# Row gathers of a graph network: no bound on the index, and no clearing of the row buffers

## The chip, the cores and the metric

The kernel runs on one core of a Trainium2 chip. The metric is device time in microseconds (us), and less is better. Engines are named as the profile names them: PE is TensorE (PEld its weight loads), DVE is VectorE, ACT is ScalarE, POOL is GpSimd and SP is SyncE; a q behind a name means that engine's sequencer.

## What is computed

Four graph layers run one after the other over 50,000 nodes of 128 features, each followed by an addition of its input and a layer norm. The edges are 25,000 random pairs in both directions, plus one loop edge per node, 100,000 in all and sorted by destination. Each layer sums rows of neighbours:

```
x = layernorm(x + gcn(x))        # two rounds:  out = D^-1/2 (A + I) D^-1/2 (x W) + b
x = layernorm(x + sage(x))       # three rounds: h W_self + mean(h[src]) W_neigh + b
x = layernorm(x + attention(x))  # sum of messages[src] * sigmoid(logit), then a GRU cell, then a batch norm
x = layernorm(x + combine(x))    # sum(x[src]) W_neigh + x W_self + b
# every sum over neighbours:  segment_sum(table[src], dst)
```

What matters here is `table[src]`: seven times, rows of a table in HBM are fetched for the 50,000 edges that are no loops. A row has 128 floats (512 B), but 256 floats (1024 B) in the second sage round and 132 floats (528 B) in the attention.

## The kernel before

**Slots.** `sort_edges` (L301) gives each of the edges that is no loop a slot. Four groups of 512 nodes make a supergroup of 2048 nodes (SG = 4); there are 25 supergroups, the last with two groups. A supergroup has K = 17 columns of 128 slots. The first 1024 edges of a supergroup fill columns 0 to 7 from the front (HALF = 8), and the rest fill columns from 16 downwards, so that what stays unfilled in a full supergroup lies in column 8 or next to it. With 2048 edges per supergroup in the mean, column 8 is nearly empty. The last supergroup uses columns 0 to 7 only. That makes 24 x 17 + 8 = 416 columns, 53,248 slots for 50,000 edges.

Of each slot, `idx` holds the row to fetch and `dcol` the node within the column's window. An unfilled slot gets no match in `dcol`, so its one-hot column is zero and whatever row lies in it is multiplied by zero. Before the change, L567 marks the unfilled slots and L570 adds NOWHERE (2^20) to their index, which is past the table's end.

**Gather stages.** Seven stages use the class `EdgeRows` (L602): `gcn_first` (tiles named g_, table t_x), `gcn_second` (g_, t_h), `sage_first` (s_, t_x), `sage_second` (s_, t_h, 256 wide), `sage_third` (s_, t_v), `attend` (at_, t_m) and `combine` (cb_, t_x). Between two stages all engines meet in a barrier (L254). In each stage:

- DVE copies the indices of the next batch into a small tile (`aim`, L646) and makes the one-hot tiles (L683), in the order of `over_groups` (L121), four groups ahead of the sums (three in the split stages, two in `attend`);
- POOL waits for that copy and issues one indirect DMA per column (`gather`, L655): 5, 5, 4 and 3 columns for the four groups of a supergroup. Each fetches 128 rows, one into each partition;
- PE multiplies rows and one-hots into a PSUM bank (L720), and the dense work of the layer follows.

The rows land in a ring of K column buffers. Stages with whole fp32 rows have two such rings (34 columns), the two split stages (`gcn_first` and `sage_second`, which part the rows into a high and a low half) one. Since a skipped row leaves the buffer as it was, DVE clears all rings at the start of a stage (`clear`, L633, called by `on_vector` at L700), and POOL waits for `cleared` before it first writes each ring. The indirect DMA is given `bounds_check=NPAD - 1` (L659), and skips rows beyond it. The bound stands in a register of POOL's sequencer, which a MOVE writes ahead of each gather.

Of the kernel before, what the change touches and what calls it, by code (L numbers as in the profile page):

```python
# [14 lines left out]
ALU = mybir.AluOpType  # L15
# [11 lines left out]
NPAD = T * GRP  # L27
LAST = NODES - (T - 1) * GRP
LASTP = LAST // BLK
SG = 4  # L30
SGN = SG * GRP
NSG = -(-T // SG)
K = 17
# [14 lines left out]
NOWHERE = 1 << 20  # L48
# [41 lines left out]
def is_first(t, slots=2):  # L90

    return isinstance(t, int) and t < slots


def wait_for(eng, sem, value):


    eng.wait_ge(sem, value)  # L98
    if not isinstance(value, int):
        eng.sem_inc(PASSED[0], 1)  # L100
# [24 lines left out]
def over_groups(eng, stages, unroll=8):  # L125


    lim = T - 2

    def step(s):  # L130
        for lag, stage in stages:
            if 0 <= s - lag < T:
                stage(Turn(None, unroll, s - lag))

    most = max(lag for lag, _ in stages)
    head = max(2 + most, unroll)
    head += (T - 2 - head) % unroll
    for s in range(head):
        step(s)
    with eng.Fori(0, (lim - head) // unroll) as j:  # L140
        for o in range(unroll):
            for lag, stage in stages:
                stage(Turn(j, unroll, head + o - lag))
    for s in range(lim, T + most):
        step(s)
# [17 lines left out]
def build_program(nc, x, src, dst, w1, b1, w2, b2, ws0, wn0, sb0, ws1, wn1, sb1, ws2, wn2, sb2,  # L163
# [4 lines left out]
    def sb(name, shape, dt=F32):  # L168
        return top.enter_context(nc.sbuf_tensor(name, shape, dt))
# [28 lines left out]
    dcol = sb("dcol", [P, SLOTS])  # L198
# [45 lines left out]
    class Phase:  # L244


        def __init__(self, ctx, name):
            self.ctx, self.name, self.own_sems = ctx, name, []
            ctx.callback(self.clear)

        def clear(self):

            nc.clear_and_free_semaphores(self.own_sems)
            nc.all_engine_barrier()  # L254
# [46 lines left out]
    def sort_edges():  # L301
# [3 lines left out]
        with ExitStack() as ctx:  # L305
            ph = Phase(ctx, "so")
# [16 lines left out]
            a, b, c = (tmp(f"a{i}", [P, CW]) for i in range(3))  # L323
# [11 lines left out]
            filled = tmp("filled", [P, SLOTS])  # L335
# [99 lines left out]
            def _(dve):  # L435
                steps = [0]

                def then(ins):

                    steps[0] += 1  # L440
                    ins.then_inc(chain, 1)
                    dve.wait_ge(chain, steps[0])

                flat = [t[:, :, :].rearrange("p b i -> p (b i)")
                        for t in (si, di, ni, sf, df, nf, ends, coded, scrap)]
# [23 lines left out]
                                         op0=ALU.mult, op1=ALU.add).then_inc(marked, 1)  # L469
# [10 lines left out]
                                              op0=ALU.mult, op1=ALU.add))  # L480
# [5 lines left out]
                                              op0=ALU.is_equal, op1=ALU.mult))  # L486
# [7 lines left out]
                                              op0=ALU.mult, op1=ALU.add))  # L494
                then(dve.scalar_tensor_tensor(out=c[:, :], in0=c[:, :], scalar=float(SGN), in1=bound[:, :],
                                              op0=ALU.add, op1=ALU.subtract))
                for n, what in enumerate((s_t, c)):
# [33 lines left out]
                                              op0=ALU.mult, op1=ALU.add))  # L531
# [3 lines left out]
                                              op0=ALU.mult, op1=ALU.add))  # L535
# [24 lines left out]
                for n in (0, 2):  # L560
# [3 lines left out]
                v = sums[:, :, :, :].rearrange("p n s f -> p (n s) f")[:, 0:SLOTS, :]  # L564
                dve.scalar_tensor_tensor(out=dsg[:, :], in0=v[:, :, 3], scalar=256.0, in1=v[:, :, 2],
                                         op0=ALU.mult, op1=ALU.add)
                dve.tensor_scalar(filled[:, :], v[:, :, 3], 0.0, None, ALU.is_equal)  # L567
                then(dve.scalar_tensor_tensor(out=dcol[:, :], in0=v[:, :, 1], scalar=256.0, in1=v[:, :, 0],
                                              op0=ALU.mult, op1=ALU.add))
                then(dve.scalar_tensor_tensor(out=dcol[:, :], in0=filled[:, :], scalar=float(NOWHERE),  # L570
                                              in1=dcol[:, :], op0=ALU.mult, op1=ALU.add))
                dve.tensor_scalar(dsg[:, :], dsg[:, :], 256.0, None, ALU.subtract)
                then(dve.tensor_scalar(dcol[:, :], dcol[:, :], 256.0, 0.0, ALU.subtract, ALU.max))
                then(dve.tensor_copy(idx[:, :], dcol[:, :]))
# [4 lines left out]
                def table(tile):  # L579
# [5 lines left out]
                                              op0=ALU.is_ge, op1=ALU.mult))  # L585
# [16 lines left out]
    class EdgeRows:  # L602
# [3 lines left out]
        def __init__(self, ph, table, width, split=False):  # L606
            self.table, self.width = table, width
            self.rings = 1 if split else 2
            self.rows = ph.tile("rows", [P, self.rings * K, width])
            if split:  # L610
                self.hi, self.lo = ph.tile("hi", [P, K, width], F32R), ph.tile("lo", [P, K, width], F32R)
            self.halves = split
            self.onehot = ph.tile("onehot", [P, K, WMAX], F32R if split else F32)
            self.index = ph.pair("index", [P, BATCHMAX], U32, n=2 * SG)
            self.cleared = ph.sem("rows_cleared")
            self.indexed = ph.sem("index_copied")
            self.gathered = ph.sems("rows_gathered", 2 * SG)
            self.split = ph.sem("rows_hi")
            self.ready = ph.sem("rows_ready")
            self.summed = ph.sem("rows_summed")  # L620
# [9 lines left out]

            return K * (q.e // SG) if self.rings == 2 else 0

        def clear(self, dve):  # L633

            for n in range(self.rings):
                dve.memset(self.rows[:, n * K:(n + 1) * K, :], 0.0).then_inc(self.cleared, 1)  # L636

        def aim(self, dve, q):

# [7 lines left out]

        def gather(self, pool, q):

            if is_first(q.t, self.rings * SG):  # L650
                pool.wait_ge(self.cleared, q.t // SG + 1)
            wait_for(pool, self.indexed, q.t + 1)
            a, b = self.batch(q)
            for k in range(a, b):
                pool.indirect_dma_start(  # L655
                    out=self.rows[:, self.ring(q) + k, :], out_offset=None, in_=self.table[0:NPAD, :],
                    in_offset=bass.IndirectOffsetOnAxis(ap=self.index[q.e][:, k - a:k - a + 1], axis=0),
                    bounds_check=NPAD - 1, oob_is_err=False).then_inc(self.gathered[q.e], 16)

        def fetch(self, pool):  # L660

# [38 lines left out]
        def on_vector(self, dve, stages, ahead=None):  # L700


            ahead = ahead or (3 if self.halves else 4)
            self.clear(dve)
            over_groups(dve, [(0, lambda q: self.aim(dve, q))] +
                        [(ahead + lag, stage) for lag, stage in stages])

# [1486 lines left out]
```

## Time and profile before

| | |
|---|---|
| median of 3 runs | 5997.48 us (5992.59 to 5998.52) |
| the profiled execution | 5996.4 us, span of its instructions 5994.6 us |
| busy share: PE, PEld, DVE, ACT, POOL | 80%, 63%, 65%, 45%, 52% |
| indirect DMAs | 7 x 416 = 2912 |
| bytes of POOL's DMA queue | 205.88 MB |
| mean granted TensorE clock | 0.928 of full |

Times in the rows are microseconds from the span's start unless they are marked ns. In a row of the timeline, the first number is the start and the second the duration; in brackets stands how long the engine was idle before it and what ended that. "issue" means that the engine waited for nothing that the profile shows.

### The profile page before, as it was taken

Reading aid. Unit: us, or ns where it says so; the run is one execution under the profiler, and the core shown is the slowest. Engines: PE = TensorE matmul, PEld = TensorE weight load, DVE = VectorE, ACT = ScalarE, POOL = GpSimd, SP = SyncE. Lnnn points to the kernel's source line nnn. Section 1 sums busy time; section 2 is a strip of 40 time slices with the busy share of each in tenths; the row PEclk is TensorE's granted clock in tenths of the full one; section 3 lists DMA queues with packets and bytes.
Section 4 is the critical chain, followed back from the end, with each engine's and each line's share of the span. In section 5 each row is a group of like instructions: output and inputs, shape, how many; then the busy total and the mean of one; then the engine's idle time right before and its main releaser. Section 6 shows DMA issues by size and latency. Waiting matters only on the chain. (4 is left out here: it accounts for less than half of the span.)

```text
span 5994.6 us, 107473 instructions
## 1 busy us (share of the span) xinstructions
PE 4806.3 (80%) x27114; PEld 3769.5 (63%) x27114; DVE 3884.4 (65%) x11826; ACT 2702.2 (45%) x6502; POOL 3119.7 (52%) x2957
## 2 busy tenths in 40 slices
PE   2208999566589998999999997777699999546887
PEld 1106888455478886777777775677566666326777
DVE  9805777566666664555555554788577777785666
ACT  0083544455622222222222222666566666694545
POOL 0007776677677754343433433777555554005776
PEclk9999999777799998999999998999899999657999
DMA  1096898444467764444444442777555555594444
GB/s 31 9 333 209 267 272 262 127 139 137 136 193 222 222 209 141 148 154 144 150 152 143 154 147 88 179 191 190 172 162 153 162 156 149 189 305 131 145 142 134
DMA packets 523175, 1010.93 MB, mean 169 GB/s; under 512 B 110803, under 2 KB 118082, under 8 KB 519962
## 3 DMA queue, kind: packets, MB, share of 16 engines
q1 hardware_dynamic: 423194, 803.47, 41.0%
q0 software_dynamic: 99840, 205.88, 14.2%
q8 instruction: 52, 0.85, 0.1%
q14 instruction: 89, 0.73, 0.0%
HBM read 686.75 MB, written 335.49 MB: 171 GB/s over the span
## 5 line engine op out<-in xcount | busy, mean ns | idle before, releaser
L655 POOL DMA_INDIRECT s_rows<-t_h,s_index x416 | 536.8, 1290 | 849.0 <-DVE s_index L646 747.9
L655 POOL DMA_INDIRECT g_rows<-t_x,g_index x416 | 444.5, 1069 | 579.9 <-DVE g_index L646 455.8
L655 POOL DMA_INDIRECT cb_rows<-t_x,cb_index x416 | 416.0, 1000 | 471.4 <-DVE cb_index L646 347.1
L655 POOL DMA_INDIRECT at_rows<-t_m,at_index x416 | 442.0, 1062 | 405.4 <-DVE at_index L646 300.8
L720 PE MATMUL bank<-s_onehot,s_rows 128*128 128x80 f32 (+9 forms) x2344 | 478.4, 358 | 154.7 <-DMA s_rows<-t_v,s_index 124.6
L720 PEld LDWEIGHTS bank<-s_onehot,s_rows 128*128 128x128 f32 x2344 | 410.4, 204 | 216.0 <-issue 89.3
L655 POOL DMA_INDIRECT s_rows<-t_v,s_index x416 | 422.6, 1016 | 214.9 <-issue 124.0
L655 POOL DMA_INDIRECT g_rows<-t_h,g_index x416 | 428.4, 1030 | 168.2 <-issue 122.2
L655 POOL DMA_INDIRECT s_rows<-t_x,s_index x416 | 425.0, 1022 | 161.4 <-issue 114.1
L720 PE MATMUL bank<-g_onehot,g_rows 128*128 128x80 f32 (+9 forms) x1172 | 307.0, 428 | 217.0 <-DMA g_rows<-t_h,g_index 194.4
L1606 DVE TENSOR_TENSOR s_rout<-bank,s_x 128x512 f32<-128x512 f32 x98 | 67.8, 692 | 586.0 <-PE bank L1550 586.0
L720 PEld LDWEIGHTS bank<-g_onehot,g_rows 128*128 128x128 f32 x1172 | 255.3, 249 | 273.1 <-issue 166.2
L1550 PEld LDWEIGHTS bank<-wuv_s,s_hid 128*128 128x128 f32 x3136 | 365.5, 192 | 47.4 <-issue 47.4
L683 DVE TENSOR_SCALAR s_onehot<-iota,dcol 128x224 f32<-128x224 f32 (+15 forms) x1248 | 380.4, 368 | 0.6
L1573 ACT ACTIVATE s_hid<-bank,sb_c 128x512 f32<-128x512 f32 x196 | 123.9, 683 | 568.3 <-PE bank L1538 568.3
L1538 PE MATMUL bank<-s_ht,ws_s 128*128 128x512 f32 x784 | 368.8, 593 | 0.0
L1538 PE MATMUL bank<-s_agg,wn_s 128*128 128x512 f32 x784 | 368.4, 592 | 0.0
L1550 PE MATMUL bank<-wuv_s,s_hid 128*128 128x128 f32 x3136 | 366.0, 275 | 0.9 <-DVE s_rout L1606 0.9
L720 PE MATMUL bank<-cb_onehot,cb_rows 128*128 128x80 f32 (+9 forms) x1172 | 244.5, 363 | 106.8 <-DMA cb_rows<-t_x,cb_index 105.2
L720 PE MATMUL bank<-g_onehot,g_hi 128*128 128x112 f32 (+9 forms) x586 | 173.1, 332 | 184.0 <-DVE g_lo L690 178.4
L720 PE MATMUL bank<-s_onehot,s_hi 128*128 128x80 f32 (+9 forms) x1172 | 288.4, 287 | 26.9 <-DVE s_lo L690 22.9
L720 PEld LDWEIGHTS bank<-cb_onehot,cb_rows 128*128 128x128 f32 x1172 | 209.1, 207 | 137.8 <-issue 74.6
(314 smaller groups left out, 12710.9 us busy)
## 6 DMA issues: line engine op xcount, KB each, us to landing
s_scale<-inv_d SPq DMA_DIRECT2D x196, 256.0 KB
t_h<-s_hout SPq DMA_DIRECT2D x98, 512.0 KB
s_own<-t_h SPq DMA_DIRECT2D x98, 512.0 KB
t_m<-s_mout SPq DMA_DIRECT2D x98, 264.0 KB
at_own<-t_m SPq DMA_DIRECT2D x98, 264.0 KB
t_x<-sx_out SPq DMA_DIRECT2D x98, 256.0 KB
g_own<-t_x SPq DMA_DIRECT2D x98, 256.0 KB
g_scale<-dinv_d SPq DMA_DIRECT2D x98, 256.0 KB
```

The source lines that it names most:

```text
L655: pool.indirect_dma_start(out=self.rows[:, self.ring(q) + k, :], out_offset=None, in_=self.table[0:NPAD, :], in_offset=bass.IndirectOffset ...
L683: last = dve.tensor_scalar(self.onehot[:, k, 0:WIDE[k]], iota[:, 0:WIDE[k]], col(dcol, q.m * K + k), None, ALU.is_equal)
L720: last = pe.matmul(to[:, a:b], part[:, at, h * P:(h + 1) * P], self.onehot[:, k, off:off + b - a], start=(i + s == 0), stop=(close and i + ...
L1538: last = pe.matmul(bank[4 + o][:, :], w[:, h, o * P:(o + 1) * P], r[q.u][:, h, :], start=(k + h == 0), stop=(k + h == 2))
L1550: last = pe.matmul(bank[6 + w][:, b * D:(b + 1) * D], hid[q.u][:, h, b * P:(b + 1) * P], wuv_s[:, h, w * D:(w + 1) * D], start=(h == 0), s ...
L1573: last = act.activation(hid[q.u][:, h, :], bank[4 + h][:, :], ACT.Relu, bias=sb1_c[:, h:h + 1])
L1606: dve.tensor_tensor(rout[q.u][:, :], bank[6][:, :], xin[q.u][:, :], ALU.add)\
```

## The change

The bound is taken off the indirect DMA, and with it everything that it needed: the two DVE operations that mark unfilled slots and push their index past the end, the clearing of the rings at the start of each of the seven stages, and POOL's wait for it. The index of an unfilled slot is now 0 (L573 takes the larger of the decoded value and 0), so row 0 of the table is fetched for it. Its one-hot column is zero as before.

```diff
                 dve.scalar_tensor_tensor(out=dsg[:, :], in0=v[:, :, 3], scalar=256.0, in1=v[:, :, 2],
                                          op0=ALU.mult, op1=ALU.add)
-                dve.tensor_scalar(filled[:, :], v[:, :, 3], 0.0, None, ALU.is_equal)
                 then(dve.scalar_tensor_tensor(out=dcol[:, :], in0=v[:, :, 1], scalar=256.0, in1=v[:, :, 0],
                                               op0=ALU.mult, op1=ALU.add))
-                then(dve.scalar_tensor_tensor(out=dcol[:, :], in0=filled[:, :], scalar=float(NOWHERE),
-                                              in1=dcol[:, :], op0=ALU.mult, op1=ALU.add))
                 dve.tensor_scalar(dsg[:, :], dsg[:, :], 256.0, None, ALU.subtract)
                 then(dve.tensor_scalar(dcol[:, :], dcol[:, :], 256.0, 0.0, ALU.subtract, ALU.max))
...
-        def clear(self, dve):
-
-            for n in range(self.rings):
-                dve.memset(self.rows[:, n * K:(n + 1) * K, :], 0.0).then_inc(self.cleared, 1)
...
         def gather(self, pool, q):
-            if is_first(q.t, self.rings * SG):
-                pool.wait_ge(self.cleared, q.t // SG + 1)
             wait_for(pool, self.indexed, q.t + 1)
             a, b = self.batch(q)
             for k in range(a, b):
                 pool.indirect_dma_start(
                     out=self.rows[:, self.ring(q) + k, :], out_offset=None, in_=self.table[0:NPAD, :],
-                    in_offset=bass.IndirectOffsetOnAxis(ap=self.index[q.e][:, k - a:k - a + 1], axis=0),
-                    bounds_check=NPAD - 1, oob_is_err=False).then_inc(self.gathered[q.e], 16)
+                    in_offset=bass.IndirectOffsetOnAxis(ap=self.index[q.e][:, k - a:k - a + 1], axis=0))\
+                    .then_inc(self.gathered[q.e], 16)
...
             ahead = ahead or (3 if self.halves else 4)
-            self.clear(dve)
             over_groups(dve, [(0, lambda q: self.aim(dve, q))] +
```

No instruction changes its place against another. At the start of `combine`, DVE's row of work began with the clearing of both rings, and then came the index copies that POOL waits for:

```order
L636 MEMSET cb_rows 128x2176 x2
L646 COPY cb_index0<-idx 128x5
L646 COPY cb_index1<-idx 128x5
L646 COPY cb_index2<-idx 128x4
L646 COPY cb_index3<-idx 128x3
L646 COPY cb_index4<-idx 128x5
```

With the change, the first index copy is DVE's first operation of the stage (the copy's line is now 642):

```order
L642 COPY cb_index0<-idx 128x5
L642 COPY cb_index1<-idx 128x5
L642 COPY cb_index2<-idx 128x4
L642 COPY cb_index3<-idx 128x3
L642 COPY cb_index4<-idx 128x5
```

## Rows read from the trace of the kernel before

**Rows 1.** By stage: us; busy PE, PEld, DVE, ACT, POOL; clock; DMA share; GB/s.

```profile
453.00:1066.00 613.00, 577.95 (x3916) 480.46 (x3916) 439.12 (x1201) 285.92 (x686) 444.54 (x416) 0.99 0.84 252
1066.00:1652.00 586.00, 358.89 (x1564) 302.37 (x1564) 372.76 (x1692) 315.56 (x980) 428.35 (x416) 0.77 0.44 132
1652.00:2256.00 604.00, 589.25 (x3126) 524.18 (x3127) 394.81 (x906) 160.64 (x195) 424.96 (x416) 0.98 0.68 211
2256.00:3675.00 1419.00, 1391.19 (x7838) 1015.18 (x7837) 750.46 (x1589) 388.41 (x589) 536.78 (x416) 0.99 0.44 146
3675.00:4272.00 597.00, 440.63 (x2735) 393.22 (x2734) 451.92 (x2082) 371.76 (x1079) 422.61 (x416) 0.91 0.66 173
4272.00:5150.00 878.00, 815.87 (x3144) 504.38 (x3143) 599.86 (x1209) 549.81 (x1299) 441.95 (x416) 0.97 0.50 149
5415.00:5995.00 580.00, 461.19 (x3132) 430.26 (x3132) 372.06 (x1702) 269.34 (x698) 415.99 (x416) 0.92 0.46 134
```

**Rows 2.** Groups of POOL's gathers: busy, mean ns, idle before, what ended it.

```profile
L655 POOL DMA_INDIRECT g_rows<-t_x,g_index x416 | 444.5, 1069 | 579.9 <-DVE g_index L646 455.8 <-issue 124.0
...
L655 POOL DMA_INDIRECT g_rows<-t_h,g_index x416 | 428.4, 1030 | 168.2 <-issue 122.2 <-DVE g_index L646 46.1
...
L655 POOL DMA_INDIRECT s_rows<-t_v,s_index x416 | 422.6, 1016 | 214.9 <-issue 124.0 <-DVE s_index L646 90.9
L655 POOL DMA_INDIRECT cb_rows<-t_x,cb_index x416 | 416.0, 1000 | 471.4 <-DVE cb_index L646 347.1 <-issue 124.3
```

**Rows 3.** Timeline of POOL at the start of combine.

```profile
5428.46 1.00 POOL L655 DMA_INDIRECT cb_rows<-t_x,cb_index  x1 [344.99 <-DVE cb_index L646]
5429.76 1.00 POOL L655 DMA_INDIRECT cb_rows<-t_x,cb_index  x1 [0.30 <-issue]
```

**Rows 4.** Timeline of the start of combine, DVE and PE.

```profile
5423.41 1.87 DVE L636 MEMSET cb_rows<- 128x2176 f32 x1 [7.00 <-issue]
...
5427.48 0.39 DVE L646 COPY cb_index<-idx 128x5 uint32<-128x5 uint32 x5
...
5436.29 3.37 PE L720 MATMUL bank<-cb_onehot,cb_rows 128*128 128x168 f32 x10 [22.51 <-DMA cb_rows<-t_x,cb_index]
```

**Rows 5.** Timeline of the starts of gcn_first and sage_second, the two stages with one ring.

```profile
455.84 1.87 DVE L636 MEMSET g_rows<- 128x2176 f32 x1 [159.40 <-PEq L254]
...
457.63 0.32 DVE L646 COPY g_index<-idx 128x5 uint32<-128x5 uint32 x4
...
2264.78 3.69 DVE L636 MEMSET s_rows<- 128x4352 f32 x1 [5.92 <-issue]
...
2268.39 0.31 DVE L646 COPY s_index<-idx 128x5 uint32<-128x5 uint32 x4
```

**Rows 6.** Timeline of DVE in sort_edges, the two operations on unfilled slots.

```profile
193.81 0.53 DVE L567 TENSOR_SCALAR so_filled<-so_value 128x425 f32<-128x425 f32 x1
...
195.20 0.60 DVE L570 SCALAR_TENSOR_TENSOR dcol<-so_filled,dcol 128x425 f32<-128x425 f32 x1
```

**Rows 7.** Line 655 alone: durations in ns, min/median/max, first and last start.

```profile
L655 POOLq MOVE  x2912: 29/29/38, 457.8 to 5953.9; - x195
L655 POOL DMA_INDIRECT g_rows<-t_x,g_index x416: 992/997/1650, 458.7 to 1028.8; - x139
...
L655 POOL DMA_INDIRECT s_rows<-t_h,s_index x416: 992/999/2927, 2269.4 to 3597.5; - x139
```

**Rows 8.** Line 655 again, in the window 5427.5 to 5435.5, the start of combine.

```profile
L655 POOLq MOVE  x15: 29/29/29, 5427.7 to 5435.5; - x15
L655 POOL DMA_INDIRECT cb_rows<-t_x,cb_index x6: 992/997/1069, 5428.5 to 5435.0; - x6
```

**Rows 9.** DMA queue of POOL: packets, MB, share of 16 engines.

```profile
q0 software_dynamic: 99840, 205.88, 14.2%
```

**Rows 10.** Same columns as rows 1; sage_first's start, loads of s_scale and own rows.

```profile
1657.40:1658.00 0.60, 0.00 (x0) 0.00 (x0) 0.60 (x4) 0.00 (x0) 0.60 (x1) 0.50 0.85 331
```

**Rows 11.** Group of POOL's small clearings: busy, mean ns.

```profile
L362 POOL MEMSET so_low<- 128x1 f32 x17 | 1.1, 88 | 0.0
```

More of the change, by code:

```diff
@@ L614, in __init__ @@
             self.index = ph.pair("index", [P, BATCHMAX], U32, n=2 * SG)
-            self.cleared = ph.sem("rows_cleared")
             self.indexed = ph.sem("index_copied")
```

## The prediction

> **What bounds the kernel now.** I read the kernel stage by stage, because the shares over the whole span mix stages with different limits. In the table by stage [rows 1], the seven gather stages take 613, 586, 604, 1419, 597, 878 and 580 us, 5277 of the span's 5994.6. PE is busy 98% of sage_first (589 of 604) and of sage_second (1391 of 1419), 93% of attend (816 of 878), but only 61%, 74% and 80% of gcn_second, sage_third and combine. gcn_first is in between (578 of 613).
>
> Next I read what POOL does in the slack stages. Its groups [rows 2] show 416.0 us busy plus 124.3 us of "issue" idle in combine, 540.3 of the stage's 580; gcn_second has 428.4 + 122.2 = 550.6 of 586, sage_third 422.6 + 124.0 = 546.6 of 597 and gcn_first 444.5 + 124.0 = 568.5 of 613. What these groups waited for an index copy is the idle time ahead of the stage. So within these four stages POOL issues gathers back to back from first to last, and a stage lasts as long as this train plus its head and its tail. The timeline [rows 3] gives the pitch: a gather of 1.00 us and 0.30 us until the next, 1.30 us each.
>
> Last I read a stage's head [rows 4]. DVE's first operation is the clearing of a ring; the first index copy starts 5427.48 - 5423.41 = 4.07 us after it; POOL's first gather starts 0.98 us after that copy [rows 3], and PE's first sum waits for the landing of the gathers, at 5436.29. Everything in the stage hangs on that copy.
>
> **The change part by part.**
>
> 1. The clearings at the heads. With two rings, the copy moves up by 4.07 us [rows 4]. With one ring it is 457.63 - 455.84 = 1.79 us in gcn_first and 2268.39 - 2264.78 = 3.61 us in sage_second, whose rows are twice as wide [rows 5]. Five stages have two rings: 5 x 4.07 + 1.79 + 3.61 = 25.8 us. Nothing else covers this time, because POOL has nothing to do before its first gather, and in the PE-bound stages PE too begins with the landing. The chain copy, gather, landing, sum moves up as a whole. DVE's one-hots move up with it and are not late.
>
> 2. Two DVE operations in sort_edges. They stand in a chain on one engine, 0.53 and 0.60 us long [rows 6]: 1.1 us.
>
> 3. The MOVE that sets the bound. There is one per gather, 29 ns, 2912 of them [rows 7]. I cost it at nothing. In the first 8 us of combine the sequencer runs 15 of them while POOL does 6 gathers [rows 8], so it is far ahead of the engine, and the pause between gathers is the same 0.30 us [rows 3] as in the rest of the stage: 124.3 / 416 = 0.30 [rows 2]. The pause is the engine's own. If the MOVE lay in it nevertheless, that would be 29 ns x 416 = 12 us in each of the four POOL-bound stages, 48 us at most, which is within what part 5 leaves open.
>
> 4. The rows now fetched. 53,248 slots less 50,000 edges leave 3248 unfilled slots. A slot costs 5 x 512 + 1024 + 528 = 4112 B over the seven stages, and 50,000 x 4112 B = 205.6 MB is what the queue moved [rows 9], so skipped rows were truly not fetched. The change adds 3248 x 4112 B = 13.4 MB. At the 252 GB/s of the stage with the most traffic [rows 1] this would be 53 us if nothing covered it. It is covered: the DMA engines are busy 44 to 84% of the stages [rows 1], the new bytes come as some 24 gathers per stage, and every gather has its 1.30 us slot anyway, in which even 64 KB take 0.2 us at the 331 GB/s seen in one stretch [rows 10]. What is not covered is the last gather of each stage, whose column is now full of rows that were skipped before: 7 x 0.2 = 1.4 us, a loss.
>
> 5. The gather's own duration. The trace of before has no gather without a bound, so this is bounded from both sides. The low end of a change is 0: the group of 1024 B rows has the same minimum and nearly the same median (992 and 999 ns) as that of 512 B rows (992 and 997 ns) [rows 7], so the duration does not follow what the rows hold, and nothing shows that a comparison is a separate piece of it. The other end is one more pass of POOL over 128 values, for which the nearest row is the clearing of one value per partition, 88 ns [rows 11]. A pass that falls away would give 0.088 x 416 = 37 us in each of gcn_second, sage_third and combine, and less in gcn_first and sage_first, where PE has only 35 and 15 us of slack [rows 1]: 110 + 35 + 15 = 160 us. If the form without a bound took a longer path instead, the same 160 us would be lost. I take 0, the value of the nearest row of the same instruction, and keep 160 us for the range.
>
> The sum: 5996.4 - 25.8 - 1.1 + 1.4 = 5970.9, so 5971 us against the profiled execution's 5996.4. That execution lies 1.1 us below the median of 5997.48, so against the median the change is 0.4%. A measurement of this kernel can tell about 0.2%, 12 us, from no change.
>
> **The rivals.**
>
> The generation gets shorter. The durations show one nearly constant value [rows 7], which would fit a loop over 128 rows in which a test is one of several steps; 997 ns / 128 is 7.8 ns per row. Against it speaks that nothing separates the test. It gives anything from 5971 down to 5971 - 160 = 5811 us. I give it 0.35, since even 10 ns per gather is felt 416 times in each POOL-bound stage.
>
> Row 0 becomes a hot spot, and the kernel gets slower. In each of 24 supergroups, nearly all of column 8's 128 slots are unfilled, so one gather asks for the same 512 B about 128 times. What the trace has of this kind are the loads of s_scale, in which all partitions read one stretch of 2048 B: while they and loads of own rows ran, 331 GB/s moved [rows 10], so that 256 KB take 0.79 us and each 512 B were read 128 times in that. A hot gather should thus land at most some 0.8 us late, and in stages with two rings the ring hides it. In gcn_first and sage_second there is one ring and PE is nearly always busy; exposed there, 48 x 0.8 = 38 us turn the gain into 5971 + 38 = 6009 us. It decides from 25.5 / 48 = 0.53 us exposed per hot gather. I give it 0.06.
>
> The Trainium skill has a rule on this side, in "DMA: Bandwidth & Descriptors", section "Latency and other measured facts": copies whose rows lie at large powers of two from each other ran at about half the rate, which it puts down, as an inference, to rows that fall on the same part of HBM. By that rule a hot gather's 0.2 us of transfer would be 0.4; were the extra 0.2 us exposed at all 168 of them, the sum would be 5971 + 34 = 6005 us. No row of this trace reads one single 512 B row 128 times, so neither is shown here.
>
> The head does not move up. If the first gather or its landing were held by something else after the barrier, such as the loads of own rows that SP issues at the same time, the 25.8 us would mostly stay, and the time would be about 5995 us. PE's first wait in combine ended with the gathered rows [rows 4], which speaks against it. 0.05.
>
> The gather without a bound takes longer, by the bound of part 5: up to 5971 + 160 = 6131 us. Nothing in the trace speaks for it. 0.04.
>
> **How the numbers follow.** My forecast has the rest, 0.50, and 5971 us is its value; its own range is 5960 to 5985. Faster by over 0.2% (under 5985) are the forecast and the shorter generation: 0.50 + 0.35 = 0.85. Within 0.2%: 0.05, the head that stays. Slower: 0.06 + 0.04 = 0.10. The range takes in the shorter generation down to its bound, 5811, and goes up to 5990, above the forecast's own upper end; it leaves out the three cases that make 0.15.
>
> **What would show it.** In the changed kernel's profile the first index copy should be DVE's first operation of each stage, with POOL's first gather 0.98 us behind it, and the stages with two rings 4 us shorter. POOL's queue should move 219 MB. The gathers' median should be 997 ns at a pitch of 1.30 us; a lower median is the first rival, and its size can be read there directly. A PE that waits longer for the rows of column 8, in gcn_first above all, would be the hot row. I am wrong if the gather's duration moves in either direction, or if the stages keep their length though the clearings are gone.

## The result, and the profile after

The changed kernel takes 5891.63 us, median of 4 runs (5887.69 to 5898.03), beside 5995.76 us for the kernel before (4 runs, 5992.59 to 5998.52): a ratio of 0.982, with an interval of 0.9808 to 0.9833. That is 104 us less. The forecast was 25 us less. The direction was right, the time lies within the range, and the gain is four times the one forecast. The profiled execution took 5898.03 us, the longest of the four, with a span of 5896.2 us, which is 98.4 us shorter than the span before.

The page of the changed kernel has 2974 instructions fewer (107,473 before), and POOL's queue moved 219.14 MB where it had moved 205.88 [rows 9]:

```profile
span 5896.2 us, 104499 instructions
...
PE 4786.1 (81%) x27114; PEld 3751.8 (64%) x27114; DVE 3866.7 (66%) x11812; ACT 2695.8 (46%) x6502; POOL 2984.4 (51%) x2957
...
q0 software_dynamic: 99840, 219.14, 16.2%
```

The gathers' line alone, which is now 649 (durations in ns, min/median/max; first and last start). It answers to [rows 7]:

```profile
L649 POOL DMA_INDIRECT g_rows<-t_x,g_index x416: 939/947/1460, 455.2 to 1014.6; - x139
L649 POOL DMA_INDIRECT g_rows<-t_h,g_index x416: 941/946/1424, 1061.1 to 1589.0; - x139
L649 POOL DMA_INDIRECT s_rows<-t_x,s_index x416: 939/947/1437, 1617.1 to 2171.7; - x139
L649 POOL DMA_INDIRECT s_rows<-t_h,s_index x416: 942/949/2863, 2225.4 to 3553.0; - x139
L649 POOL DMA_INDIRECT s_rows<-t_v,s_index x416: 941/947/1446, 3638.9 to 4165.4; - x139
L649 POOL DMA_INDIRECT at_rows<-t_m,at_index x416: 939/1016/1343, 4210.3 to 5006.1; - x139
L649 POOL DMA_INDIRECT cb_rows<-t_x,cb_index x416: 941/947/1110, 5346.1 to 5869.5; - x139
```

The same view of the kernel before, the five stages that [rows 7] leaves out:

```profile
L655 POOL DMA_INDIRECT g_rows<-t_h,g_index x416: 992/997/1487, 1071.6 to 1625.3; - x139
L655 POOL DMA_INDIRECT s_rows<-t_x,s_index x416: 991/997/1482, 1657.1 to 2211.7; - x139
...
L655 POOL DMA_INDIRECT s_rows<-t_v,s_index x416: 992/997/1497, 3687.0 to 4235.1; - x139
L655 POOL DMA_INDIRECT at_rows<-t_m,at_index x416: 991/1001/1311, 4285.4 to 5082.4; - x139
L655 POOL DMA_INDIRECT cb_rows<-t_x,cb_index x416: 992/997/1120, 5428.5 to 5969.8; - x139
```

The median of a gather fell from 997 to 947 ns. That is the first thing to see, and it is what the prediction had named as the sign of its first rival. The second thing is in the start times. From them this table is worked out: a train is the time from a stage's first gather to its last; an interval runs from a stage's first gather to the first gather of the next stage, and from that of combine to the end of the span.

| Stage | train before | train after | interval before | interval after | less |
|---|---|---|---|---|---|
| gcn_first | 570.1 | 559.4 | 612.9 | 605.9 | 7.0 |
| gcn_second | 553.7 | 527.9 | 585.5 | 556.0 | 29.5 |
| sage_first | 554.6 | 554.6 | 612.3 | 608.3 | 4.0 |
| sage_second | 1328.1 | 1327.6 | 1417.6 | 1413.5 | 4.1 |
| sage_third | 548.1 | 526.5 | 598.4 | 571.4 | 27.0 |
| attend | 797.0 | 795.8 | 1143.1 | 1135.8 | 7.3 |
| combine | 541.3 | 523.4 | 566.1 | 550.1 | 16.0 |

The intervals lose 94.9 us, and the time ahead of the first gather goes from 458.7 to 455.2 us. Together that is 98.4, the whole difference of the spans. Every interval but the last holds the next stage's head. What is left above that is in three trains: 25.8 us in gcn_second, 21.6 in sage_third and 17.9 in combine, 65.3 us together. The busy times by stage (columns as in [rows 1]) show why it is these three:

```profile
450.00:1056.00 606.00, 577.07 (x3916) 481.74 (x3916) 444.73 (x1198) 280.63 (x691) 415.29 (x416) 0.99 0.85 257
1056.00:1612.00 556.00, 349.48 (x1564) 294.02 (x1564) 374.34 (x1693) 313.77 (x978) 402.31 (x416) 0.77 0.48 142
1612.00:2221.00 609.00, 590.31 (x3132) 524.57 (x3132) 391.87 (x906) 163.34 (x200) 403.41 (x416) 0.98 0.70 214
2221.00:3634.00 1413.00, 1390.82 (x7832) 1014.60 (x7832) 745.86 (x1589) 387.56 (x588) 526.47 (x416) 0.99 0.45 148
3634.00:4206.00 572.00, 438.69 (x2740) 391.67 (x2740) 449.62 (x2086) 371.56 (x1078) 400.92 (x416) 0.91 0.71 185
4206.00:5076.00 870.00, 812.95 (x3132) 502.36 (x3132) 594.20 (x1204) 550.03 (x1299) 433.58 (x416) 0.98 0.52 152
5340.00:5896.00 556.00, 455.54 (x3132) 423.46 (x3132) 364.55 (x1690) 267.62 (x692) 397.86 (x416) 0.93 0.50 143
```

gcn_second, sage_third and combine are the stages where POOL set the time and PE is busy 349 of 556, 439 of 572 and 456 of 556 us. The groups of POOL's gathers (busy, mean ns, idle before) tell the same. The first row is gcn_first, which is read further down; the last three are these stages, which lost busy time and kept their pauses, about 124 us of "issue" each as in [rows 2]:

```profile
L649 POOL DMA_INDIRECT g_rows<-t_x,g_index x416 | 415.3, 998 | 594.9 <-DVE g_index L642 485.5 <-issue 109.4
...
L649 POOL DMA_INDIRECT g_rows<-t_h,g_index x416 | 402.3, 967 | 172.1 <-issue 124.7 <-DVE g_index L642 47.4
L649 POOL DMA_INDIRECT s_rows<-t_v,s_index x416 | 400.9, 964 | 211.5 <-issue 124.1 <-DVE s_index L642 87.4
L649 POOL DMA_INDIRECT cb_rows<-t_x,cb_index x416 | 397.9, 956 | 465.5 <-DVE cb_index L642 342.7 <-issue 122.8
```

Beside [rows 2], the busy time of these three fell by 26.1, 21.7 and 18.1 us, 65.9 together, which is what the trains lost. In the mean a gather is 63, 52 and 44 ns shorter, in the median 50 or 51. Part of the spread is in the long gathers: in gcn_second 42 took over 1.1 us before and 19 after. No run tells why these became fewer.

The start of combine on the timeline (start and duration in us, idle before in brackets) answers to [rows 3] and [rows 4]:

```profile
5345.63 0.45 DVE L642 COPY cb_index<-idx 128x5 uint32<-128x5 uint32 x5 [6.51 <-PEq L254]
...
5346.07 1.04 POOL L649 DMA_INDIRECT cb_rows<-t_x,cb_index  x1 [339.00 <-DVE cb_index L642]
...
5347.41 0.94 POOL L649 DMA_INDIRECT cb_rows<-t_x,cb_index  x1 [0.30 <-issue]
...
5353.74 2.52 PE L713 MATMUL bank<-cb_onehot,cb_rows 128*128 128x168 f32 x6 [17.26 <-DMA cb_rows<-t_x,cb_index]
```

DVE's last operation of the stage before ended 5345.63 - 6.51 = 5339.12 us, and the first gather starts 6.95 us later. Before, it was 5423.41 - 7.00 = 5416.41, and 12.05 us later [rows 3, 4]. The head is 5.10 us shorter, where 4.07 had been forecast.

In sort_edges, DVE's chain no longer holds the two operations of [rows 6]. From the operation ahead of them to the one behind them it took 2.86 us and takes 194.77 - 193.01 = 1.76, so 1.1 us less:

```profile
193.01 0.91 DVE L565 SCALAR_TENSOR_TENSOR dsg<-so_value 128x425 f32<-128x425 f32 x1
193.84 0.90 DVE L568 SCALAR_TENSOR_TENSOR dcol<-so_value 128x425 f32<-128x425 f32 x1
194.77 0.38 DVE L571 TENSOR_SCALAR dsg<-dsg 128x425 f32<-128x425 f32 x1
```

### The profile page after: what moved, and what is told of

The parts are those of the page before. It is cut to its first block and busy times, and to the rows that moved or that the text cites. A ratio compares the mean times of both kernels' runs of the same rounds, so it can differ in the third digit from the quotient of the medians.

```text
span 5896.2 us, 104499 instructions
## 1 busy us (share of the span) xinstructions
PE 4786.1 (81%) x27114; PEld 3751.8 (64%) x27114; DVE 3866.7 (66%) x11812; ACT 2695.8 (46%) x6502; POOL 2984.4 (51%) x2957
## 3 DMA queue, kind: packets, MB, share of 16 engines
q0 software_dynamic: 99840, 219.14, 16.2%
## 5 line engine op out<-in xcount | busy, mean ns | idle before, releaser
L649 POOL DMA_INDIRECT s_rows<-t_h,s_index x416 | 526.5, 1266 | 854.9 <-DVE s_index L642 753.5
L649 POOL DMA_INDIRECT g_rows<-t_x,g_index x416 | 415.3, 998 | 594.9 <-DVE g_index L642 485.5
L649 POOL DMA_INDIRECT cb_rows<-t_x,cb_index x416 | 397.9, 956 | 465.5 <-DVE cb_index L642 342.7
L649 POOL DMA_INDIRECT s_rows<-t_v,s_index x416 | 400.9, 964 | 211.5 <-issue 124.1
L649 POOL DMA_INDIRECT s_rows<-t_x,s_index x416 | 403.4, 970 | 179.3 <-issue 121.4
L649 POOL DMA_INDIRECT g_rows<-t_h,g_index x416 | 402.3, 967 | 172.1 <-issue 124.7
L713 PE MATMUL bank<-s_onehot,s_hi 128*128 128x80 f32 (+9 forms) x1172 | 288.4, 287 | 22.1 <-DVE s_lo L684 18.1
L713 PE MATMUL bank<-s_onehot,s_lo 128*128 128x80 f32 (+9 forms) x1172 | 285.0, 285 | 0.0
```

The source lines that it names most:

```text
L649: pool.indirect_dma_start(out=self.rows[:, self.ring(q) + k, :], out_offset=None, in_=self.table[0:NPAD, :], in_offset=bass.IndirectOffset ...
L713: last = pe.matmul(to[:, a:b], part[:, at, h * P:(h + 1) * P], self.onehot[:, k, off:off + b - a], start=(i + s == 0), stop=(close and i + ...
```

## The experiments

The theory after the result: a bound on the index adds 50 ns to a gather's own work on POOL (called the test here), which the three stages bound by POOL feel 416 times each; the clearings cost what their heads show. The rivals: it was the MOVE between the gathers; it was the skipping of rows; the clearings gave more than their heads; and row 0 as a hot row eats part of the gain.

### Each half of the change alone

The clearings and the wait on them put back into the changed kernel, without a bound (e9; e1 is the same kernel on another chip):

```diff
+            if is_first(q.t, self.rings * SG):
+                pool.wait_ge(self.cleared, q.t // SG + 1)
...
+            self.clear(dve)
             over_groups(dve, [(0, lambda q: self.aim(dve, q))] +
```

The bound put back, without clearings (e10; e2 is the same kernel on another chip). Here unfilled slots still hold index 0, so the bound is compared and never skips a row:

```diff
-                    in_offset=bass.IndirectOffsetOnAxis(ap=self.index[q.e][:, k - a:k - a + 1], axis=0))\
-                    .then_inc(self.gathered[q.e], 16)
+                    in_offset=bass.IndirectOffsetOnAxis(ap=self.index[q.e][:, k - a:k - a + 1], axis=0),
+                    bounds_check=NPAD - 1, oob_is_err=False).then_inc(self.gathered[q.e], 16)
```

> The clearings put back once more, since the first run of this kernel came from a chip on which the kernel before itself took 6806 us. Theory A (no bound makes each gather 50 ns shorter, the heads are worth 25.8 us): 947 ns, 5892 + 26 = 5918 us, a ratio of 0.987. Rival B (the clearings are worth most of the gain): 5970 us or more.

> The bound put back once more, for the same reason. Theory A: 997 ns; three stages bound by POOL lose 0.050 x 416 = 21 us each and gcn_first about 10, so 5892 + 73 = 5965 us, a ratio of 0.995. Rival C (skipping, not testing, was slow): 5892 us, which the 1000 ns of the first run already speak against.

Measured: on that chip the kernel before took 6000.48 us. e9 took 5922.89 us (5921.3 to 5928.42, 4 runs), ratio 0.9871 (0.9856 to 0.9886). e10 took 5968.27 us (5965.66 to 5976.4, 5 runs), ratio 0.9949 (0.9936 to 0.9963). Combine's gathers in e9 and in e10, with the MOVE of e10:

```profile
L658 POOL DMA_INDIRECT cb_rows<-t_x,cb_index x416: 940/944/1112, 5376.4 to 5897.4; - x139
```

```profile
L649 POOLq MOVE  x2912: 29/29/38, 454.0 to 5923.6; - x195
...
L649 POOL DMA_INDIRECT cb_rows<-t_x,cb_index x416: 992/997/1173, 5397.6 to 5939.7; - x139
```

Both expectations were met. The duration follows the bound and not the clearings: 944 ns with clearings and without a bound, 997 ns with a bound and without clearings. Leaving the bound out is worth 6000.48 - 5922.89 = 78 us, leaving the clearings out 6000.48 - 5968.27 = 32 us. The two ratios multiply to 0.9871 x 0.9949 = 0.982, the ratio of the whole change. In us the halves make 110, where the change gave 104. The sort's 1.1 us are counted in both, and the rest lies within their intervals, which are 8 to 9 us to either side. A second comparison on the same chip is e11, further down, which has neither half and took 5886.09 us: from there the clearings cost 37 us and the bound 82.

In e10 no row is skipped, so it is not the skipping that costs, but the bound being there at all. e10 is also the change as the forecast had it, shorter heads and the old gather. Its 5968 us lie 3 us beside the forecast's 5971, and by its ratio, which takes out the chip, it would be 5965.

### A chip on which PE was held back

The first four runs went to another chip, where the kernel before itself took 6805.89 us (6786.63 to 6828.48, 29 runs). e3 has the bound, set once per stage instead of once per gather:

```diff
+            with pool.register(f"bound_{self.rows.name}") as self.bound:
+                pool.reg_mov(self.bound, NPAD - 1)
+                over_groups(pool, [(0, lambda q: self.gather(pool, q))])
```

e4 sends the unfilled slots to rows of their own, row 25344 plus the partition's number in place of row 0:

```diff
+                dve.tensor_scalar(filled[:, :], v[:, :, 3], 0.0, None, ALU.is_equal)
...
+                then(dve.scalar_tensor_tensor(out=dcol[:, :], in0=filled[:, :], scalar=e_f[:, LEAD + 200:LEAD + 201],
+                                              in1=dcol[:, :], op0=ALU.mult, op1=ALU.add))
```

> The changed kernel with the clearings at the stage heads and POOL's wait for them put back; no bound, and row 0 for unfilled slots, as in the changed kernel. Theory A (the gather itself is 50 ns shorter without a bound, and that is the part of the gain I did not forecast): the gathers' median stays at 947 ns and only the heads' 25.8 us come back, so 5892 + 26 = 5918 us, about 0.987 of before. Rival B (the clearings cost far more than the heads, since DVE's writes disturb what follows): most of the 104 us come back, 5970 us or more.

> The changed kernel with the bound put back on the gather (and its MOVE with it); unfilled slots still ask for row 0, so nothing is ever skipped, and nothing is cleared. Theory A: the gathers' median is 997 ns again and the time is what I had forecast for the change, 5971 us. Rival C (the longer gather of before came from skipping rows, not from testing them): the median stays at 947 ns and the time at 5892 us.

> As the run before, but the bound's register is set once at the start of a stage instead of ahead of each gather, so that the bound is tested and no MOVE stands between gathers. Theory A (the test inside the gather): 997 ns and 5971 us, with the pause of 0.30 us unchanged. Rival D (the MOVE costs the time): 947 ns or a shorter pause, 5892 us.

> The changed kernel, but the unfilled slot of partition p asks for row 25344 + p instead of row 0, with the two DVE operations back that this needs (1.1 us). Theory A: no hot spot is exposed, 5892 + 1 = 5893 us. Rival E (hot row): the gathers of column 8, which land some 0.8 us late in the changed kernel's trace, land like the others, and where there is one ring this shows, up to 48 x 0.8 = 38 us less, 5855 us.

Measured: e1 (clearings, no bound) 6821.85 us, ratio 1.0027 (1.0011 to 1.0044); e2 (bound, no clearings) 6770.78 us, 0.9957 (0.994 to 0.9974); e3 (bound in one register, no clearings) 6756.98 us, 0.9927 (0.9907 to 0.9948); e4 (neither, spread rows) 6792.82 us, 0.9977 (0.9965 to 0.999). The durations came as expected: 944 ns in e1 and e4, 1000 ns in e2 and e3. The times did not, since all were set for chips like the first; and relative to the kernel before, e1 and e4 failed, which should have gained most and gained nothing or little. Combine's gathers in e1 and in e3:

```profile
L658 POOL DMA_INDIRECT cb_rows<-t_x,cb_index x416: 938/944/1089, 6039.6 to 6767.4; - x139
```

```profile
L649 POOL DMA_INDIRECT cb_rows<-t_x,cb_index x416: 994/1000/1119, 5996.2 to 6725.9; - x139
```

A stretch of e1's combine, with the columns of [rows 1], and PE's timeline in it:

```profile
6072.00:6092.00 20.00, 3.45 (x8) 2.51 (x9) 0.00 (x0) 0.00 (x0) 12.27 (x13) 0.50 0.19 46
```

```profile
6079.62 0.29 PE L723 MATMUL bank<-cb_onehot,cb_rows 128*128 128x80 f32 x1 [2.51 <-issue]
6082.42 0.49 PE L723 MATMUL bank<-cb_onehot,cb_rows 128*128 128x196 f32 x1 [2.51 <-issue]
```

On this chip a gather was shorter by the same 56 ns (944 against 1000), but combine's train took 728 us in e1 and 730 in e3, not 521 and 542: POOL no longer set the stage. In e1 it waited 546 us for combine's index copies, 344 of them ahead of the stage, so 202 us within it. There were stretches in which PE began one matmul every 2.8 us, waiting for nothing that the profile shows, at a granted clock of 0.50. What held PE there is not known. With the stages waiting for PE, a shorter gather gained nothing. It even went with a loss: 16 us from the kernel before to e1, and 22 us from e2 to e4, and I have no cause for that. The heads kept their worth (35 us from the kernel before to e2, 29 us from e1 to e4). All other runs are from chips on which the kernel before took 5992 to 6000 us.

### The MOVE

e3 already bears on it: it has 104,506 instructions, seven more than the changed kernel, so the 2912 MOVEs of the kernel before are down to one per stage, and its gathers still take 1000 ns. So the MOVE is not what made them long. Nor does it lie in the pause, which at the start of e3's combine is what it was:

```profile
5995.76 0.45 DVE L642 COPY cb_index<-idx 128x5 uint32<-128x5 uint32 x5 [6.50 <-PEq L254]
...
5996.20 1.12 POOL L649 DMA_INDIRECT cb_rows<-t_x,cb_index  x1 [338.51 <-DVE cb_index L642]
...
5997.62 1.09 POOL L649 DMA_INDIRECT cb_rows<-t_x,cb_index  x1 [0.30 <-issue]
```

But the same rows show where the MOVE does cost: ahead of a stage's first gather. Here that gather starts 5996.20 - 5995.76 = 0.44 us after the copy, as in the changed kernel. In e10, with a MOVE per gather, it starts 5397.57 - 5396.59 = 0.98 us after it:

```profile
5396.59 0.46 DVE L642 COPY cb_index<-idx 128x5 uint32<-128x5 uint32 x5 [6.51 <-PEq L254]
...
5397.57 1.05 POOL L649 DMA_INDIRECT cb_rows<-t_x,cb_index  x1 [337.06 <-DVE cb_index L642]
```

Over the seven stages, the time from POOL's last branch ahead of a stage to its first gather sums to 9.3 us in e2 and to 6.9 in e3, which differ in nothing but the MOVEs. So they cost 2.4 us in all. e3 took 14 us less than e2, but the two intervals overlap.

e5 was to add the MOVE back ahead of each gather of the changed kernel, without a bound:

```diff
             for k in range(a, b):
+                pool.reg_mov(self.bound, NPAD - 1)
                 pool.indirect_dma_start(
```

> The changed kernel with one idle MOVE of a constant into a register of POOL's sequencer ahead of each gather, as the bound needed it; no bound. Theory A: nothing changes, 947 ns, pause 0.30 us, 5892 us. Rival D (the MOVE costs time): 29 ns x 416 = 12 us more in each stage bound by POOL, up to 48 us in all.

Measured: 5886.32 us (5881.22 to 5893.75, 4 runs), ratio 0.9825 (0.9808 to 0.9841) against 5992.36 us. Its page, and its gathers in combine:

```profile
span 5879.4 us, 104499 instructions
```

```profile
L650 POOL DMA_INDIRECT cb_rows<-t_x,cb_index x416: 940/944/1100, 5334.4 to 5855.0; - x139
```

The number of instructions tells that this kernel did not do what its edit says: 104,499 is exactly that of the changed kernel, and no MOVE stands in its trace. A MOVE into a register that nothing reads did not get into the program. e5 is thus a repeat of the change on another chip (0.9825 beside 0.982), and says nothing of the MOVE. What clears the MOVE of the 50 ns is e3: with 2912 MOVEs [rows 3], with seven, and with none, the pause is 0.30 us, and the duration goes with the bound.

### What in the bound costs

e6 keeps the comparison and takes the form that reports an index out of bounds, where before it was skipped:

```diff
+                    bounds_check=NPAD - 1, oob_is_err=True).then_inc(self.gathered[q.e], 16)
```

e7 and e8 gather only the rows of partitions 0 to 63, with the bound and without it; both have the clearings. The rows of partitions 64 to 127 are left out of their sums:

```diff
+                    out=self.rows[0:64, self.ring(q) + k, :], out_offset=None, in_=self.table[0:NPAD, :],
+                    in_offset=bass.IndirectOffsetOnAxis(ap=self.index[q.e][0:64, k - a:k - a + 1], axis=0),
```

> The changed kernel with the bound put back, but in the form that reports an index beyond it instead of skipping the row (no index is beyond it). Theory A1 (the comparison costs the 50 ns): 997 ns. A2 (only the form that may skip costs them): 947 ns.

> The kernel before, but each gather fetches only the rows of partitions 0 to 63; the rows of the other half are left out (zero). Together with the next run it tells whether the 50 ns are a cost per row or per gather. If all of the gather's time is per row: 997 / 2 = 499 ns. If the time per gather is mostly fixed: near 997 ns.

> The changed kernel with the clearings put back, and each gather fetches only the rows of partitions 0 to 63; the rows of the other half are left out (zero). If the bound costs a fixed 50 ns per gather, the gather is 50 ns shorter than in the run before; if it costs 50 / 128 = 0.39 ns per row, 25 ns shorter.

Measured, one execution each: e6 6000.18 us, e7 5908.21, e8 5861.73. Combine's gathers in each of the three:

```profile
L649 POOL DMA_INDIRECT cb_rows<-t_x,cb_index x416: 1006/1010/1162, 5425.6 to 5973.7; - x139
```

```profile
L655 POOL DMA_INDIRECT cb_rows<-t_x,cb_index x416: 938/942/1114, 5361.4 to 5882.2; - x139
```

```profile
L658 POOL DMA_INDIRECT cb_rows<-t_x,cb_index x416: 899/903/1022, 5330.8 to 5834.0; - x139
```

The reporting form is dearer still, 1010 ns against 944, so the bound costs in either form, and not in the skipping form alone; the 997 ns expected of it were 13 too few. With half the rows a gather without a bound takes 903 ns instead of 944, and one with a bound 942 instead of 997. A row costs 41 / 64 = 0.64 ns without the bound and 55 / 64 = 0.86 ns with it. The bound thus costs 53 ns at 128 rows and 39 ns at 64, between the 50 and the 25 that the expectation had for a cost per gather and one per row. By the line through these two points, an estimate, it is 25 ns per gather and 0.22 ns per row. That a gather is a loop over 128 rows of 7.8 ns each, as the first rival's text had put it, is wrong: all but 82 of its 944 ns stay however many rows there are, as far as two sizes tell.

### The hot row

e11 is e4's kernel again, on a chip with a free PE. e12 sends every slot of every gather to row 0, by clearing all indices; the sums then add up row 0, and the real sums over neighbours are left out:

```diff
-                then(dve.tensor_copy(idx[:, :], dcol[:, :]))
+                then(dve.memset(idx[:, :], 0))
```

> Unfilled slots ask for 128 different rows once more, for the same reason. Theory A (the hot row lands about 0.8 us late, but nothing waits for it): 5892 + 1 = 5893 us, equal to the changed kernel. Rival E (it is exposed where there is one ring): 5855 to 5885 us, and gcn_first shorter by 10 us or more.

> Every index is set to 0, so that all 416 gathers of every stage fetch row 0 into all 128 partitions; the sums over neighbours are left out by this. It asks what the hot row costs if it is made 17 times as frequent. If a hot gather only lands 0.8 us late and does not hold the queue: POOL's trains keep their length and the time stays within 30 us of 5892 us. If reads of one row are served one after the other and a hot gather occupies that row's memory for more than the pitch of 1.25 us: landings fall behind from gather to gather, and the stages with 416 gathers grow by a multiple, above 6300 us.

Measured: e11 took 5886.09 us (5879.76 to 5890.34, 5 runs), ratio 0.9807 (0.9794 to 0.9821), whose interval overlaps that of the change (0.9808 to 0.9833). Its gcn_first and gcn_second, to be read beside the first two rows of the changed kernel's stages:

```profile
456.00:1059.00 603.00, 575.78 (x3916) 480.45 (x3916) 445.06 (x1196) 279.48 (x686) 414.82 (x416) 0.99 0.86 258
1059.00:1614.00 555.00, 355.23 (x1564) 298.90 (x1564) 375.48 (x1696) 315.38 (x980) 400.86 (x416) 0.76 0.47 142
```

e12 took 7486.13 us (one execution). Its queue, then its gcn_second and combine, and last combine's gathers:

```profile
q0 software_dynamic: 99840, 219.14, 52.7%
```

```profile
1452.00:2258.00 806.00, 429.38 (x1564) 342.30 (x1564) 366.06 (x1690) 317.56 (x980) 397.76 (x416) 0.67 0.95 98
6671.00:7484.00 813.00, 527.11 (x3132) 478.97 (x3132) 366.55 (x1687) 272.13 (x686) 393.42 (x416) 0.83 0.95 97
```

```profile
L649 POOL DMA_INDIRECT cb_rows<-t_x,cb_index x416: 938/944/1113, 6671.1 to 7431.1; - x139
```

Row 0 is a hot row: when all gathers want it, the same 219.14 MB take 52.7% of the DMA engines in 7484 us instead of 16.2% in 5896, 4.1 times the time. Combine's train is 760 us, 1.83 us per gather, and the engines are busy 95% of it. For 64 KB this is 36 GB/s. The time is 7486 us, above the 6300 that the expectation had set, though no stage grew by a multiple.

In the changed kernel only one gather in some 17 is of this kind. From the semaphore events in the trace I worked out when the gathers of column 8 landed after their start (medians, over the groups whose events are all in the trace). In gcn_second that went from 2.27 us (rows skipped) to 3.51, and in combine from 2.23 to 3.89, where e11 has 2.52 and 2.55. In sage_second, whose rows are 1024 B, it went from 2.32 to 3.54, where e11 has 2.73. So the hot row lands 0.8 to 1.3 us later than spread rows.

Nothing waits for it that a run could show. The two stages with one ring, where the rival had it strike, tell this best. From first gather to first gather, gcn_first takes 605.9 us in the changed kernel and 603.4 in e11; but e5, which is the changed kernel over again and has the hot row, takes 600.7. sage_second takes 1413.5 in the changed kernel, 1413.6 in e5 and 1412.9 in e11. Combine takes 550.1, 545.0 and 545.9. So the small differences are not the row's, and rival E's 10 us in gcn_first did not come.

The bound saves some 78 us and the clearings 32, which within the intervals is the whole change. No version ran that beats the changed kernel by more than the intervals can tell.

## Why the prediction was right in direction and off in size

**The gather's own duration, part 5: the step that failed.** It had the gain bounded by 0 and 88 ns per gather and took 0, "the value of the nearest row of the same instruction". The change measured 50 ns (997 to 947), the halves of it 53 (997 to 944). Over 415 gathers from the first to the start of the last, 50 ns are 21 us in each of three stages, 62 us of the 65 us that the three trains lost. The reasoning was at fault, not only the size: that rows of 512 B and of 1024 B take equally long [rows 7] says that a gather's duration does not follow the bytes of a row. It says nothing of a test that both kinds carry. Nothing in the trace of before could size the test; but with a sensitivity of 1250 us per us of gather in the three stages, and bounds of 0 and 88 ns, the end at 0 was the one value that could hardly be exact. The middle of the bounds, 44 ns, would have given 5971 - 55 = 5916 us. That this lies near what was measured is luck, since the 88 ns are those of another instruction, a clearing. That the measured time lies within the stated range is owed to this wide bound too; the forecast's own range, 5960 to 5985, it missed.

**The caps of part 5.** It allowed 35 us for gcn_first and 15 us for sage_first, the slack of PE there. Neither came. gcn_first's train is 10.7 us shorter, but its interval only 7.0, and the next head alone gives 4.9 of these. In the rest after the last gather PE is busy 38.52 of 44 us, where before it was 30.05 of 40:

```profile
1012.00:1056.00 44.00, 38.52 (x261) 31.47 (x259) 28.24 (x76) 21.38 (x59) 2.92 (x3) 0.99 0.76 237
```

So it seems that work which POOL had kept waiting was done later, at the end. POOL's waits for the index copy (us in all, times, the longest), after and before, tell the same:

```profile
POOL g_rows L649 <- DVE g_index L642: 532.8, 64, 449.8
```

```profile
POOL g_rows L655 <- DVE g_index L646: 501.9, 24, 453.4
```

The longest is the one ahead of the stage. Without it, gcn_first's gathers waited 485.5 - 449.8 = 35.7 us, and 455.8 - 453.4 = 2.4 before [rows 2]. So 33 us are new: POOL, now faster, waits for DVE's copy, and DVE makes it behind its other work of the stage. In sage_first POOL's train did not move at all, 554.6 us before and after. The slack of PE over a whole stage, 35 and 15 us, was here no measure of what a faster POOL brings.

**The heads, parts 1 and 3.** Forecast 25.8 us. By the trace, the times from POOL's last branch ahead of each stage to its first gather sum to 39.0 us before and 6.5 after, so 32.5. The same sum is 9.3 us in e10 and 38.5 in e9. So the clearings alone are worth 29.7 us (with the sort's 1.1 that is 30.8, beside the 32 measured for e10), the bound alone 0.6, and a further 2.2 came only with both gone. The clearing's 4.07 us was right. What part 1 missed is how soon DVE starts: in combine its first operation after the barrier comes 0.49 us sooner as a copy than as a clearing (6.51 against 7.00). What part 3 missed is the MOVE, which it costed at nothing because the sequencer is far ahead of the engine. That holds between gathers, but ahead of a stage's first gather it has no lead: the gather follows the copy after 0.98 us with the MOVE (before, e2, e10) and after 0.44 without it (e3 and the changed kernel, combine), 2.4 us over the seven stages. In e9, where POOL waits for the clearing at the same place, it is 0.90 us, so either half alone keeps most of this time.

**Parts 2 and 4, and the rest of part 3.** The sort's 1.1 us came as forecast. Between gathers the MOVE costs nothing, as argued. The queue moves 219.14 MB, the forecast 219, and they are hidden as forecast. The 1.4 us for the last gathers can't be told apart: after combine's last gather the span lasts 26.7 us, 24.8 before.

The sum by what was measured is 32.5 (heads) + 1.1 (sort) + 65.3 (three trains) = 98.9 us, beside 98.4 in the spans. What the sum leaves out, such as gcn_first's shorter train and longer rest, is at most some 2 us in a stage either way and cancels.

**The rivals.** The shorter generation, which had 0.35, is what happened; its signs were the right ones, its picture of equal steps per row was not. The hot row exists, and its extra 0.8 us were close to the 0.8 to 1.3 us seen, but it is not exposed: gcn_first and sage_second, where it was to strike, took at most 1 us more in e5, with it, than in e11, without it. That its price was close is luck, for it was taken from a row that misled. The loads of s_scale [rows 10] read one stretch at 331 GB/s, and 128 reads of one row run at 36. The kernel in which every gather is hot pays some 1590 us for it.

The Trainium skill's rule in "DMA: Bandwidth & Descriptors", section "Latency and other measured facts", is on rows at large powers of two from each other and says about half the rate. No run here has such a pitch. For many reads of one row, the runs show worse than its half, a factor of 4.1 in the engines' time, and where it is one gather in 17 they show no loss.

**The head that stays, and the longer gather** did not come: every first gather moved up, and no gather without a bound takes longer than 949 ns in the median but those of attend, at 1016 beside 1001, in a stage that PE sets.

## What to carry to other kernels

Where an engine issues the same instruction back to back and thereby sets a stage, an optional field of that instruction may be on the critical path, as the bound was here; price it by an experiment before anything else, and until then don't take the end of its bounds that is convenient. Then check that another engine isn't nearly full in that stage: in sage_first, where PE is busy 590 of 609 us, the shorter gather gained nothing, and on the chip that held PE back e1 gained nothing at all. A small instruction that is free in a full queue can cost at the start of a stage, as the MOVE did. And count the instructions of an experiment before reading its time: an edit may not have got into the program.

## What the runs showed of the hardware that was not expected

- A gather's time on POOL depends little on the number of its rows: 944 ns for 128 (e9) and 903 for 64 (e8), with 0.30 us of pause behind either. The bound adds 53 and 39 ns; the form that reports an index out of bounds adds 66 at 128 rows (e6).
- The MOVE that sets the bound is free between gathers, and costs up to 0.54 us ahead of a stage's first one (e2 and e10 against e3).
- POOL's time for a gather is not that of its data. With all rows hot (e12) it stays 944 ns while combine's gathers follow each other every 1.83 us. This agrees with the Trainium skill, "Perfetto Trace Analysis", section "DMA Instruction — SWDGE (GPSIMD)", by which the instruction's end in the profile is the end of the writing of descriptors.
- 128 reads of one row of 512 B run at 36 GB/s, with the DMA engines 95% busy (e12, combine).
- One chip ran the kernel before in 6806 us, others in 5992 to 6000. There PE began one matmul every 2.8 us for stretches, at a granted clock of 0.50, in the stages where it had slack; sage_second, where it is nearly always busy, kept its length (1328 us from first to last gather in the kernel before, 1333 in e1).
